# Transformer stage: in steps 0, 4 and 7 ScalarE takes the exponential first, not behind the inversions and copies

## The reference, cut to what matters

```python
def attn_layer(x, Wqkv, qs, ksc, Wo):
    qkv = x @ Wqkv                       # 16 heads of 64
    q, k, v = heads(qkv)
    q = l2norm(q) * qs;  k = l2norm(k) * ksc
    q = q * cos * scale + rotate_half(q) * sin * scale
    k = k * cos * inv + rotate_half(k) * sin * inv
    out = local_attention(q, k, v)       # windows of 32, each sees itself and the one before
    return out @ Wo

def ffn_layer(x, g, bln, W1, b1, W2, b2):
    xn = (x - mu) / jnp.sqrt(var + 1e-05) * g + bln
    a, gate = jnp.split(xn @ W1 + b1, 2, -1)
    return a * jax.nn.gelu(gate, approximate=False) @ W2 + b2

for i in range(6):
    x = attn_layer(shift_tokens(x), Wqkv[i], q_scale[i], k_scale[i], Wo[i]) + x
    x = ffn_layer(shift_tokens(x), ln_g[i], ln_b[i], W1[i], b1[i], W2[i], b2[i]) + x
```

## Time and profile before

| | |
|---|---|
| median of 3 runs | 3710.39 us (3702.64 to 3718.77) |
| the profiled execution's own time | 3709.09 us |
| its span, first to last instruction | 3707.4 us |
| PE busy (matmuls) | 2992.1 us, 81% |
| DVE busy | 2466.2 us, 67% |
| ACT busy | 2083.8 us, 56% |
| POOL busy | 1285.4 us, 35% |
| mean granted clock of TensorE | 0.906 of full speed |

### The profile page before, as it was taken

The page is one execution under the profiler, slowest core; times in us unless marked ns, Lnnn a source line. Parts: engine busy times, 40 slices in busy tenths (PEclk is TensorE's granted clock), DMA queues, the critical chain, the costliest instruction groups (busy, mean ns, idle before and its releaser), DMA issues. The chain is left out here.

```text
span 3707.4 us, 71470 instructions
## 1 busy us (share of the span) xinstructions
PE 2992.1 (81%) x22883; PEld 1620.1 (44%) x22883; DVE 2466.2 (67%) x4021; ACT 2083.8 (56%) x3805; POOL 1285.4 (35%) x1223
## 2 busy tenths in 40 slices
PE   2688887239738888845999999999999999999997
PEld 1332332113312223313665565566556556655653
DVE  6788888562347777765666666666666666666664
ACT  1477677112204666633666666666666666666664
POOL 0000000004323556624553354345435434544540
PEclk6588789569957999977999999999999999999998
DMA  5221121114231111232111111111111111111111
GB/s 197 84 85 55 62 73 60 56 45 108 67 38 30 35 34 34 37 68 99 38 54 31 49 54 31 42 45 51 34 49 49 35 42 45 49 31 53 38 35 42
DMA packets 195211, 200.31 MB, mean 54 GB/s; under 512 B 119077, under 2 KB 125877, under 8 KB 190090
## 3 DMA queue, kind: packets, MB, share of 16 engines
q1 hardware_dynamic: 193778, 195.46, 19.2%
q10 hardware_dynamic: 1080, 0.25, 0.0%
HBM read 99.84 MB, written 29.46 MB: 35 GB/s over the span
## 5 line engine op out<-in xcount | busy, mean ns | idle before, releaser
L2421 POOL TENSOR_TENSOR tr_t<-tr_t 128x512 f32<-128x512 f32 x384 | 489.7, 1275 | 683.5 <-DVE tr_t L2259 683.5
L2428 POOL TENSOR_TENSOR tr_nq<-tr_t,tr_rn 128x512 f32<-128x512 f32 x384 | 392.2, 1042 | 366.5 <-ACT tr_rn L2155 362.7
L1638 DVE TENSOR_REDUCE attn_mp<-attn_ps 128x1 f32<-128x512 f32 (+3 forms) x664 | 397.3, 656 | 146.4 <-PE attn_ps L1498 76.5
L2258 DVE TENSOR_TENSOR tr_t<-tr_ps,tr_tab 128x512 f32<-128x512 f32 x384 | 263.2, 685 | 241.1 <-ACT tr_sq L2129 241.1
L1957 PE MATMUL tr_ps<-tr_w,tr_xs 128*128 128x512 f32 x768 | 372.5, 607 | 25.0 <-DVE tr_xs L2292 21.8
L684 DVE TENSOR_REDUCE attn_mcol<-attn_ps 128x1 f32<-128x512 f32 x548 | 357.3, 681 | 50.2 <-PE attn_ps L529 40.4
L1600 ACT ACTIVATE attn_pr<-attn_ps 128x768 f32<-128x768 f32 (+2 forms) x352 | 294.9, 868 | 142.3 <-PE attn_ps L1521 140.0
L2143 ACT ACTIVATE tr_rd<-tr_ps 128x384 f32<-128x384 f32 x264 | 129.0, 489 | 376.1 <-PE tr_ps L1976 375.9
L1943 PEld LDWEIGHTS tr_ps<-tr_qT,tr_kT 64*128 64x128 f32 x4224 | 258.5, 188 | 176.6 <-issue 174.9
L1943 PE MATMUL tr_ps<-tr_qT,tr_kT 64*128 64x96 f32 (+1 forms) x4224 | 301.2, 282 | 31.4 <-ACT tr_kT L2164 20.1
L668 ACT ACTIVATE attn_pr<-attn_ps 128x512 f32<-128x512 f32 x512 | 272.6, 600 | 87.1 <-DVE attn_ps L706 68.9
(11 more groups left out here) (257 smaller groups left out, 5177.0 us busy)
## 6 DMA issues: line engine op xcount, KB each, us to landing
tr_v<-tr_va SPq DMA_DIRECT2D x144, 192.0 KB, 2.6
attn_ka<-scratch_kp SPq DMA_DIRECT2D x72, 294.0 KB
tr_v<-tr_va SPq DMA_DIRECT2D x144, 128.0 KB, 2.2
moe_cb<-scratch_combineT SPq DMA_DIRECT2D x32, 512.0 KB
tr_w<-in_w_half SPq DMA_DIRECT2D x12, 1024.0 KB
tr_v<-tr_va SPq DMA_DIRECT2D x48, 256.0 KB, 2.4
scratch_kp<-proj_parts SPq DMA_DIRECT2D x36, 256.0 KB
attn_km<-scratch_kp SPq DMA_DIRECT2D x72, 98.0 KB
```

Of the source, the lines that this page charges most:

```text
L1638: dve.tensor_reduce(dst, src, AX.X, ALU.max).then_inc(maxed, 1)
L2258: dve.tensor_tensor(out[0], product, table[0], ALU.mult)
L2421: pool.tensor_tensor(t12[:, slot, i, 0, :], t12[:, slot, i, 0, :], t12[:, slot, i, 1, :], ALU.add).then_inc(summed, 1)
L2428: pool.tensor_tensor(nq[:, slot, i, :].rearrange("p (h e) -> p h e", e=DH), t12[:, slot, i, 0, :].rearrange("p (h e) -> p h e", e=DH), rn[ ...
```

## The change

ScalarE's exps(s) is called at the head of its step in steps 0, 4 and 7, ahead of invert, roots and copy_turned. In all other steps it stays where it was, behind them. No other engine's list is touched.

```diff
 OUT_AT = {3: 0, 5: 1, 7: 2, 9: 3}
+SHORT = (0, 4, 7)
...
                 for s in range(NQT):
+                    if s in SHORT:
+                        exps(n, j, s)
                     if s:
                         invert(n, s - 1)
                     elif not first:
...
                         squares(n + 1, PROJ_NEXT_AT[s])
                         copy_v(n + 1, PROJ_NEXT_AT[s])
-                    exps(n, j, s)
+                    if s not in SHORT:
+                        exps(n, j, s)
                     if feeding:
                         feed_step(s, 2 * L if j == 3 else 2 * L - 1)
```

## The result

The changed kernel takes 3973.9 us (median of 4 runs, 3955.0 to 3975.5) against 3711.0 (4 runs of the kernel before): a ratio of 1.070, 95% interval 1.068 to 1.072. The prediction was 3957 us, range 3845 to 4000.

What follows compares the result with a forecast made beforehand. The prediction took TensorE to set the pace, released by ScalarE's queue order. To the profiled 3709.1 us it added 143 us of delays and 104 us of lower clock, 3956, given as 3957 us; range 3845 to 4000.

Steps and rivals of the forecast that it cites:

- The delay of invert: ScalarE's queue, steps 0, 4 and 7: waiting for the mask delays invert, the copies and PE alike, +143 us.
- No gain: Denominators on TensorE: exp(7) already ends 1.38 us early, and the 29.4 us of exponential waits lie elsewhere, so 0 us.
- The clock: TensorE behind the 67 longer pauses: most are followed by a fall to the lower clock, +104 us, bounds 0 and 138.
- one in ten: Share of TensorE's 67 new pauses taken to pass without a fall of the clock, leaving 104 us.
- the 45 pauses outside the feeding steps: TensorE's new pauses in steps 0, 4 and 7 without feed-forward: 2.06 us a fall, 93 us before the one-in-ten allowance.
- the 22 feeding steps 0 and 4: Steps with feed-forward work: slower matmuls partly fill up's waits for the gates, so 1 us each, 22 us before the allowance.
- Delays without falls: Rival on TensorE's clock: pauses grow but the stage's mean clock stays at 0.99, 3852 us; chance 0.15.
- Absorption: Rival on VectorE: it catches up and makes masks earlier, leaving a third of both costs, 3792 us; chance 0.08.
- The other side: Rival on PE's exponential waits: early ones free the denominators, 29.4 us could go, 3680 us; chance 0.02 faster, 0.02 within 0.5%.

Runs made afterwards that it cites:

- filled pauses: The changed kernel plus 4 or 5 matmuls with constants in PE's long pauses of steps 0, 4 and 7, outside passes with j = 1: 3857.9 us, ratio 1.040.
- step 7 alone: Against the kernel before, the exponential goes to the head of ScalarE's queue in step 7 only, not in steps 0 and 4: 3792.2 us, ratio 1.022.
- the exponential behind invert: Against the changed kernel, in steps 0, 4 and 7 the exponential goes behind invert but ahead of the roots and copies: 3862.6 us, ratio 1.041.

## Why the prediction was right

The mechanism was right in both parts. Of the 264 us that the profiled execution lost, 148 are pauses (143 predicted), 108 are busy time at the lower clock (104), and 8 come from ahead of the stage, which the prediction has no term for.

- **The delay of invert.** Predicted 2.14 us in step 7; in the timeline invert starts 4.53 us into the step (2320.70 - 2316.17) against 2.40, so 2.13. The pauses in the stage grew by 148 us in the trace, 148.8 in the table of waits; predicted 143. Step 7 brought 50.2 (51), step 4 without feed-forward 21.1 (22), step 4 with it 27.6 (28). Step 0 brought 41.0 in the 19 passes that I counted (42), and 8.8 in the five that I counted at nothing: 7.2 at the loop's edges and 1.6 in the very first. At the edge the mask is early, but the exponential still stands ahead of invert and the copies:

```profile
2187.03 0.84 ACT L2121 ACTIVATE tr_pr<-tr_pr 128x768 f32<-128x768 f32 x1 [3.31 <-DVE tr_pr L2270]
2187.19 1.09 PE L1997 MATMUL tr_ps<-ident,tr_nq 128*128 128x128 f32 x8
2187.78 0.47 ACT L2144 ACTIVATE tr_rd<-tr_ps 128x384 f32<-128x384 f32 x1
```

This is step 0 of pass 5 in the changed kernel. The denominators end at 2186.80 and the mask at 2187.00, so invert could have started near 2186.84: in the kernel before it starts 0.04 us behind the denominators there. It starts 0.94 us later, and most of that is the exponential itself. The step has a pause of 1.93 us where there was none, and is 1.5 us less busy, since more of it ran at 1.2 GHz before. It takes 8.0 us against 7.57, so the price in time there is some 0.5 us.
- **No gain.** Right: the waits for exponentials didn't change by a tenth of a microsecond.
- **The clock.** Predicted 104 us, measured 108 us of added busy time in the stage's stretch. The filled pauses show that the cause is the pauses. Up to the last step the trace's record of the clock holds 59 stretches at 1.2 GHz, 276 us in all, against 4 with 20 us before. That the number is so close is luck: two errors cancel. Of the 67 grown pauses 54 were followed by a fall, one in five without and not one in ten. So the 45 pauses outside the feeding steps cost less than the 83 us that the prediction comes to: busy time grew by 69.4 us in these steps and the ones behind them, 1.5 each. The 24 steps 7 with the steps 8 behind them are 39.4 us of it, 1.64 each. In the 22 feeding steps 0 and 4, which I put at 1 us because waits of up would hide the slower matmuls, 20 us in all, busy time grew by 41.9 us, 1.9 each. The two sum to 111 us, and 3 us less comes out mostly because none of the pauses at the loop's edges was followed by a fall this time. The waits for the gates are too short to hide slower matmuls: 0.7 us at most. Step 4 of pass 11 shows it. The stretch in the kernel before, with the columns of the earlier trace rows:

```profile
2630.01:2640.58 10.57, 9.07 (x57) 4.78 (x56) 5.40 (x9) 7.50 (x13) 3.31 (x3) 1.00 0.12 35
```

And in the changed kernel:

```profile
2753.51:2769.51 16.00, 11.99 (x58) 5.97 (x57) 5.49 (x9) 7.49 (x13) 3.32 (x3) 0.79 0.07 23
```

Of 5.43 us more, 2.92 are busy time and 2.51 are pause, as predicted for the pause alone.
- **The rivals.** Delays without falls: refuted by 108 us of busy time and a stage clock of 0.94, and the run with filled pauses shows what it would have looked like, 3858 us against the 3852 given. Absorption: refuted, except that most of the delay goes once VectorE's order makes the mask early. The other side: no wait for an exponential went. Its price was real, though, and the run that moves exponentials of other steps collected it.

## What to carry to other kernels

Moving an instruction to the head of an engine's queue moves its wait there too: compare when its input is ready with when the instructions behind it could start, and ask who stands idle for those. Look first at which waits name the instruction and in which steps they lie: here exp of steps 2, 6, 8 and 10 was late and exp of steps 0, 4 and 7 was not. When PE's pauses grow to two or three microseconds, price the lower clock behind them as well; here it was two fifths of the loss.

## What the runs showed of the hardware

The granted clock doesn't follow the length of a pause alone. Counting the pauses of PE over 1.3 us in the stage against the record of the clock: of the 24 pauses of 2.8 to 2.9 us in step 7, 18 were followed by a fall in the changed kernel, and 13 with step 7 alone. Of the 24 pauses of 1.9 to 2.0 us in step 7 of the run with the exponential behind invert it was 13, and of the 11 feeding steps 0 there, at 2.24 us, all. Even the four pauses at the loop's edges, each with a fall in the kernel before, had one fall with step 7 alone, and none in the changed kernel. Pauses up to 1.6 us had none in any run: 24 with step 7 at 1.4 to 1.6 us where the mask was early, and 24 in step 4 of the kernel before.

Whether this is also behind the scatter of the runs (3955.0 to 3975.5 us for the changed kernel, 3780.1 to 3800.2 with step 7 alone) isn't shown: the kernel before scatters by 17 us too, 3701.4 to 3718.8, and one execution of each kernel was profiled. What the Trainium skill says of repeated pauses (TensorE: Matmul & The Clock Gate, section "HAM oscillation — how this bites in real kernels"), that the price is paid at each of them, holds here for most pauses and not for all, 54 of the 67 grown ones in the changed kernel. What decides for a single pause was not tried.
